# Local attention layers: the last inverse norms move from ScalarE's square root to VectorE, and the first tile's softmax moves forward

## The chip, the cores and the metric

The kernel runs on one core of a Trainium2 chip. The metric is the device time of one execution in microseconds; the time before is the median of three runs. Five engines matter, and each works through its own queue of instructions in order: TensorE (PE), VectorE (DVE), ScalarE (ACT), GpSimd (POOL) and SyncE (SP), which only issues DMAs. They meet through semaphores: an instruction may raise one when it is done, and a wait in a queue holds everything behind it in that queue.

## The reference, cut to what matters

The program computes two large layers for a batch of 4 sequences of 1024 tokens of width 128. The part that the change touches stands in the gate branch of the second layer: two local attention layers (`DEPTH = 2`), each with 8 heads of 64 channels and windows of 64 tokens that also see the window before.

```python
qkv = h @ wqkv
q, k, v = to_heads(split(qkv))
q = l2norm(q) * qs                       # q / max(|q|, 1e-12), for each token and head
k = l2norm(k) * ksc
q, k = rotary_xpos(q, k)
sim = einsum('bhwid,bhwjd->bhwij', q * 8, look_around(k))
attn = softmax(where(mask, -max, sim))   # 64 queries, 128 keys
o = einsum('bhwij,bhwjd->bhwid', attn, look_around(v))
x = x + o @ wo                           # then a GEGLU feed-forward part
```

The four sequences are worked one after the other and each passes two local layers, so the changed stretch runs 8 times in an execution.

## The kernel before, in words

A local layer is cut into T = 8 tiles of 128 tokens. It has two loops on each engine, written out by hand, and the order of the code is the order of each queue.

**The projection loop, tiles t = 0 to 7.** TensorE's `qkv(t)` multiplies a tile by the three weight blocks into two banks of PSUM for q and k and one for v. VectorE's `rotate(t)` multiplies q and k by the cosine and sine tables (lines 1228 and 1235), and GpSimd adds the two products (line 536). ScalarE squares q and k (line 746) and copies v out (line 747). VectorE sums the squares of each head (line 1260, its result `ssq`), and after every second tile takes the maximum with a floor (line 1265). ScalarE takes the square root of two tiles' sums (line 751), and VectorE's `inverse(k)` makes a reciprocal of it and one Newton step (lines 1242 to 1245). Only the keys need the inverse norm in place: GpSimd multiplies them by it (line 542). The queries' inverse norm is applied later, as the scale of the exponential. TensorE's `kq(t)` transposes a finished tile into two banks, first the queries' half, then the keys' half (line 1734), and ScalarE's `keep(t)` copies both halves out (lines 733 and 735). `kq(t)` runs four tiles behind the projection (`LAG = 4`), and each half of it waits until `keep(t - 1)` has emptied its bank.

**The score loop, u = 0 to 11.** TensorE's `scores(u)` first adds the mask and then multiplies queries by keys (both told as line 1412, as all its matmuls are). VectorE's `top(u)` takes the maximum of each row (line 1274) and multiplies it by minus the inverse norm (line 1276). ScalarE runs eight exponentials for a tile, one per head, each with its sum (line 765). VectorE then divides by the sums (lines 1301 and 1303), TensorE transposes the weights (line 1817), ScalarE and VectorE copy them out (lines 773 and 1329), TensorE multiplies by the values and by `wo`, and VectorE adds the result to x (line 1309).

**The seam between the two loops** is where the change lies. Before, ScalarE's queue there holds: `keep(2)`, square and v of tile 7, `keep(3)`, square root of tiles 6 and 7, a one-element exponential that brings in the exponential's table (line 753), `keep(4)`, the exponentials of tile 0, `keep(5)`, the exponentials of tile 1, `keep(6)`, and so on (`LATE = 3` tiles are kept within the score loop). VectorE's queue holds: rotation of tile 7, inverse norms of tiles 4 and 5, sums of squares of tiles 6 and 7, maximum with the floor, `top(0)`, inverse norms of tiles 6 and 7, `top(1)`. TensorE's queue holds: `qkv(7)`, `kq(3)`, `scores(0)`, `kq(4)`, `scores(1)`, `kq(5)`, `scores(2)`, `kq(6)` (`EARLY = 2`). GpSimd's queue holds: keys of tile 4, rotation sum of tile 7, keys of tiles 5, 6 and 7.

The exponentials' output `pl` lies in three buffers over the same memory as the rotated tiles 2, 3 and 4 (`qk_a`), which is free once their transposes are done.

Of the kernel before, what the change touches and what calls it, by code (L numbers as in the profile page):

```python
# [7 lines left out]
ACT = mybir.ActivationFunctionType  # L8
# [3 lines left out]
AX = mybir.AxisListType.X  # L12

B, N, W = 4, 1024, 128
P = 128
T = N // P
# [50 lines left out]
def build(nc, d, out):  # L67

    with ExitStack() as ctx:
# [489 lines left out]
        def _(act):  # L559
# [21 lines left out]
            with nc.Fori(0, B, engines=(act.engine,), hint_back_edge=True, head_slot={act.engine: 0}) as b:  # L581
# [139 lines left out]
                for l in range(DEPTH):  # L721
# [7 lines left out]
                    def keep(t):  # L729
# [5 lines left out]
                        act.copy(kT[:, :, WIN + P * t:WIN + P * t + P],  # L735
                                 PS[:, 7, :].rearrange("p (c n) -> p c n", c=4)).then_inc(S["kq"], 1)

                    for t in range(T + LAG + 1 - LATE):
                        u = l * T + t
                        if t >= LAG + 1:  # L740
                            keep(t - LAG - 1)
                        if t < T:
                            act.wait_ge(S["rotb"], u + 1)
                            if u >= 2:
                                act.wait_ge(S["ssq"], u - 1)
                            act.activation(qk_sq[l][t % 2], pair(2 * (t % 2)), ACT.Square).then_inc(S["sq"], 1)  # L746
                            act.copy(vl[:, t], PS[:, 4 + t % 2, :]).then_inc(S["vl"], 1)  # L747
                        if 2 <= t <= T and t % 2 == 0:
                            k = t - 2
                            act.wait_ge(S["ssq_ok"], u // 2)  # L750
                            act.activation(rq[:, k:k + 2], rqt[:, k:k + 2], ACT.Sqrt).then_inc(S["rq0"], 1)
                        if t == T:
                            act.activation(sc[0:1, 9:10], ident[0:1, 0:1], ACT.Exp)
                    for u in range(T + 4):
                        n = T * l + u
                        if u < T:
                            if 1 <= u <= LATE:
                                keep(T - LATE + u - 1)
                            act.wait_ge(S["ml"], n + 1)
                            if n >= 3:  # L760
                                act.wait_ge(S["pt_ps"], 2 * (n - 2))
                            for r in range(2):
                                for c in range(4):
                                    h = 2 * c + r
                                    act.activation(pl[:, n % 3, r, c], PS[:, 2 * (n % 2) + r, KEYS * c:KEYS * c + KEYS],  # L765
                                                   ACT.Exp, bias=ml[:, n % 2, r, c:c + 1], scale=rq[:, u, h:h + 1],
                                                   accum_out=sl[:, n % 3, r, c:c + 1]).then_inc(S["p_exp"], 1)
                        if 2 <= u <= T + 1:
                            m = n - 2
                            if m >= 2:  # L770
                                act.wait_ge(S["o_lps"], m - 1)
                            act.wait_ge(S["pt_ps"], 2 * m + 1)
                            act.copy(pt[:, m % 2, 0], PS[:, 4, :].rearrange("p (c n) -> p c n", c=4)).then_inc(S["pt"], 1)  # L773
                        if 3 <= u <= T + 2:
                            q = n - 3
                            act.wait_ge(S["o_lps"], q + 1)
                            if q >= 2:
                                act.wait_ge(S["ol_ps"], q - 1)
                            act.copy(olT[:, q % 2], PS[:, 6, :].rearrange("p (c n) -> p c n", c=4))\  # L779
                                .then_inc(S["olT"], 1)  # L780
# [26 lines left out]
        def _(dve):  # L807
# [120 lines left out]
            with nc.Fori(0, B, engines=(dve.engine,), hint_back_edge=True, head_slot={dve.engine: 0}) as b:  # L928
# [287 lines left out]
                for l in range(DEPTH):  # L1216
# [21 lines left out]
                    def inverse(k):  # L1238

                        y, v, w = rq[:, k:k + 2], rqt[:, k:k + 2], ssq[:, k:k + 2]  # L1240
                        dve.wait_ge(S["rq0"], (l * T + k) // 2 + 1)
                        link(dve.reciprocal(y, y))
                        link(dve.scalar_tensor_tensor(w, y, -0.5, y, ALU.mult, ALU.mult))
                        link(dve.tensor_tensor(w, w, v, ALU.mult))
                        dve.scalar_tensor_tensor(y, w, 1.5, y, ALU.add, ALU.mult).then_inc(S["rqe"], 2)

                    for t in range(T + 1):
                        u = l * T + t
                        if t < T:
                            rotate(t)  # L1250
                        if l == 0 and t == 0:
                            rows_back(1)
                        if l == 0 and t == 1:
# [8 lines left out]
                        if 2 <= t and t % 2 == 0:  # L1262
# [4 lines left out]
                    def top(u):  # L1267

                        n = T * l + u
                        sv = PS[:, 2 * (n % 2):2 * (n % 2) + 2, :].rearrange("p r (c k) -> p r c k", k=KEYS)  # L1270
                        dve.wait_ge(S["s_lps"], n + 1)
                        if n >= 2:
                            dve.wait_ge(S["p_exp"], 8 * (n - 1))
                        link(dve.tensor_reduce(ml[:, n % 2], sv, AX, ALU.max))  # L1274

                        dve.scalar_tensor_tensor(ml[:, n % 2], ml[:, n % 2], -1.0,
                                                 rq[:, u, 0:HL].rearrange("p (c r) -> p r c", r=2),
                                                 ALU.mult, ALU.mult).then_inc(S["ml"], 1)

                    top(0)  # L1280
                    inverse(T - 2)

                    def own_half(t):

# [11 lines left out]
                    for u in range(T + 6):  # L1296
                        n = T * l + u
                        if 2 <= u <= T + 1:
                            m = n - 2
                            dve.wait_ge(S["p_exp"], 8 * (m + 1))  # L1300
                            link(dve.reciprocal(rl[:, m % 3], sl[:, m % 3]))
                            v = pl[:, m % 3]
                            dve.tensor_tensor(v, v, bc(rl[:, m % 3], [P, 2, 4, KEYS], 3), ALU.mult).then_inc(S["pn"], 1)
                        if 1 <= u < T:
                            top(u)
                        if u >= 6:
# [103 lines left out]
        def _(pe):  # L1410
# [22 lines left out]
            with nc.Fori(0, B, engines=(pe.engine,), hint_back_edge=True, head_slot={pe.engine: 0}) as b:  # L1433
# [277 lines left out]
                for l in range(DEPTH):  # L1711
# [52 lines left out]
                    for t in range(T):  # L1764
# [13 lines left out]
                            out_products()  # L1778
                        if l == 0 and t == 3:
                            pe.wait_ge(S["op_rd"], 1)  # L1780
                        if t >= LAG:
                            kq(t - LAG)
                    for t in range(EARLY):
                        scores(t)
                        kq(T - LAG + t)
                    for u in range(T + 4):
                        n = T * l + u
# [22 lines left out]
                        if 2 <= u <= T + 1:  # L1810
                            m = n - 2
                            pe.wait_ge(S["pn"], m + 1)
                            for r in range(2):
                                if m:
                                    pe.wait_ge(S["ptd" if r else "pt"], m)
                                for c in range(4):
                                    ins = pe.transpose(PS[:, 4 + r, P * c:P * c + P], pl[:, m % 3, r, c], ident[:])
# [197 lines left out]
```

## Time and profile before

| what | value |
|---|---|
| median of 3 runs | 2427.04 us (2421.03 to 2428.21) |
| profiled execution, its own time | 2423.78 us |
| its span, first to last instruction | 2421.7 us |
| mean granted TensorE clock | 0.939 |
| busy: PE, DVE, ACT, POOL | 86%, 78%, 60%, 25% |

The span is what the trace covers; the 2.1 us between it and the execution's own time lie around the program. A granted clock of 1.00 is 2.4 GHz, 0.50 is 1.2 GHz. In rows of a timeline the bracket tells how long the engine sat idle ahead of the instruction and what ended that. All times of a timeline are microseconds from the span's start. The first local layer of the first sequence, which the rows below show, runs from about 414 to 520 us.

### The profile page before, as it was taken

To read this page: it belongs to the slowest core of one execution; us is meant where nothing else is said; L and a number is where in the kernel's file an instruction comes from. 1 tells how busy PE (TensorE), PEld (TensorE's weight loads), DVE (VectorE), ACT (ScalarE), POOL (GpSimd) and SP (SyncE) were. 2 spreads that over 40 slices of the span, in tenths; PEclk is the share of its full clock that TensorE was granted. 3 is DMA by queue.
4 is the path that set the end of the run, shared out by engine and by line. 5 is a ranking of instruction groups with operands and counts; after the bars stand their busy time and mean duration, and the time that the engine had idled before them with its cause. 6 is when DMAs were issued, how large, how long until landed. Compare 5 with 4: busy or idle time off the path is not lost.

```text
span 2421.7 us, 49342 instructions
## 1 busy us (share of the span) xinstructions
PE 2072.6 (86%) x18320; PEld 1204.0 (50%) x18320; DVE 1894.7 (78%) x3719; ACT 1456.9 (60%) x3090; POOL 602.0 (25%) x480
## 2 busy tenths in 40 slices
PE   5997899787799699978779969987788996998877
PEld 4675233556467423364647733336464772334645
DVE  7746998887765699878776579987877558998786
ACT  4333698748334379784733438967563344996765
POOL 2632000332252200124134310031504330004050
PEclk9999799999899789999989979999998996999999
DMA  4001200100000210101000031010100003001010
GB/s 159 1 1 53 55 12 11 30 21 19 19 1 1 77 33 9 21 21 32 16 10 1 1 86 27 9 30 12 33 14 9 1 1 93 20 12 34 5 34 22
DMA packets 63896, 63.28 MB, mean 26 GB/s; under 512 B 22000, under 2 KB 49200, under 8 KB 63152
## 3 DMA queue, kind: packets, MB, share of 16 engines
q1 hardware_dynamic: 60472, 57.27, 9.4%
q8 instruction: 148, 2.42, 0.4%
q10 hardware_dynamic: 3192, 2.90, 0.4%
q14 instruction: 84, 0.69, 0.1%
HBM read 24.68 MB, written 15.01 MB: 16 GB/s over the span
## 4 chain that ended last, share of the span: by engine, by line
PE 52%; DVE 22%; ACT 17%; issue 5%; DMA 2%; SPq 1%; POOL 0%; DVEq 0%; ACTq 0%
PE PS L1412 50%; ACT arena L765 9%; DVE arena L1150 3%; DVE arena L1260 2%; ACT arena L708 2%; DVE s_at L1235 1%; DVE arena L1228 1%; PE PS L1430 1%; DMA tmp<-xf 1%; DVE tmp L1235 1%; ACT arena L773 1%; DVE arena L1353 1%; ACT arena L733 1%; ACT arena L735 1%; ACT x_in L779 1%
## 5 line engine op out<-in xcount | busy, mean ns | idle before, releaser
L1412 PE MATMUL PS<-arena 128*32 128x256 f32 (+5 forms) x11328 | 788.8, 327 | 115.2 <-DVE arena L1150 24.2
L1412 PEld LDWEIGHTS PS<-arena 128*32 128x32 f32 (+5 forms) x11328 | 349.1, 118 | 554.0 <-ACT arena L708 203.0
L1150 DVE TENSOR_REDUCE arena<-PS 128x2 f32<-128x1024 f32 x512 | 592.5, 1216 | 29.5 <-PE PS L1412 28.3
L708 ACT ACTIVATE arena<-PS 128x512 f32<-128x512 f32 x944 | 513.2, 596 | 93.2 <-PE PS L1412 69.5
L661 ACT ACTIVATE arena<-PS 128x512 f32<-128x512 f32 x256 | 150.7, 597 | 244.2 <-PE PS L1412 244.1
L1412 PEld LDWEIGHTS PS<-w2e,arena 128*128 128x128 f32 x2048 | 246.0, 192 | 50.7 <-issue 49.8
L1113 DVE TENSOR_TENSOR arena<-PS,arena 128x512 f32<-128x512 f32 x128 | 86.2, 688 | 208.5 <-PE PS L1412 208.1
L1412 PE MATMUL PS<-w2e,arena 128*128 128x128 f32 x2048 | 247.7, 275 | 0.3
L765 ACT ACTIVATE arena<-PS,arena 128x128 f32<-128x128 f32 x512 | 236.5, 626 | 0.0
L511 POOL TENSOR_TENSOR zz<-zz,arena 128x512 f32<-128x512 f32 x104 | 135.2, 1300 | 265.6 <-DVE arena L1113 236.7
L1412 PE MATMUL PS<-wqkv,arena 128*128 128x512 f32 x384 | 176.8, 598 | 21.7 <-ACT arena L747 21.7
L765 ACT ACTIVATION_READ_ACCUMULATOR arena<-PS,arena 128x1 f32 x512 | 176.2, 374 | 0.0
L520 POOL CAST arena<-arena 128x32 bf16<-128x32 f32 x64 | 13.4, 209 | 624.4 <-DVE arena L1169 624.4
L547 POOL TENSOR_TENSOR tmp<-xf,b2f 128x1024 f32<-128x1024 f32 x8 | 18.8, 2355 | 422.3 <-ACT xT L785 422.3
L1412 PE MATMUL PS<-xT,w1e 128*128 128x512 f32 x256 | 120.5, 596 | 0.2
L1412 PE MATMUL PS<-x,w1e 128*128 128x512 f32 x256 | 120.5, 596 | 0.1
L1412 PEld LDWEIGHTS PS<-wqkv,arena 128*128 128x128 f32 x384 | 67.8, 190 | 97.5 <-issue 75.8
L500 POOL TENSOR_TENSOR arena<-arena 128x1024 f32<-128x1024 f32 x32 | 75.2, 2349 | 131.3 <-ACT arena L610 122.6
L1412 PE MATMUL PS<-xT,wf 128*128 128x512 f32 (+1 forms) x192 | 89.8, 597 | 3.8 <-ACT xT L785 3.8
L746 ACT ACTIVATE arena<-PS 128x1024 f32<-128x1024 f32 x32 | 32.7, 1023 | 97.4 <-DVE s_at L1235 97.4
L1274 DVE TENSOR_REDUCE arena<-PS 128x8 f32<-128x1024 f32 x64 | 78.2, 1223 | 10.8 <-PE PS L1412 10.6
L1412 PE MATMUL PS<-xT,vw 128*128 128x512 f32 x128 | 77.6, 737 | 9.2 <-ACT arena L598 9.2
(308 smaller groups left out, 3301.1 us busy)
## 6 DMA issues: line engine op xcount, KB each, us to landing
arena<-arena SPq DMA_DIRECT2D x120, 128.0 KB, 2.3
scr_q<-arena SPq DMA_DIRECT2D x40, 128.0 KB, 2.4
scr_k<-arena SPq DMA_DIRECT2D x40, 128.0 KB, 2.4
arena<-scr_k SPq DMA_DIRECT2D x24, 200.0 KB
arena<-scr_q SPq DMA_DIRECT2D x24, 192.0 KB
scr_m<-arena SPq DMA_DIRECT2D x256, 1.0 KB
x_in<-in_x SPq DMA_DIRECT2D x5, 512.0 KB, 4.5
arena<-scr_m SPq DMA_DIRECT2D x128, 2.0 KB
```

What stands on the lines that cost most here:

```text
L500: pool.tensor_tensor(ub[:, c % 2], vsb[:, c % 2], bsb[:, c % 2], ALU.mult).then_inc(S["ub"], 1)
L511: pool.tensor_tensor(zz[:, half], src[:, half], ym[:, m % 4], ALU.add).then_inc(S["z"], 1)
L661: act.activation(hs[:, n % 8], PS[:, up_bank("up", k, c), :], ACT.Silu).then_inc(S["hs"], 1)
L708: act.activation(pb[:, n % 8, HALF * r:HALF * r + HALF], PS[:, (2 * n + r) % 3, :], ACT.Exp)\
L746: act.activation(qk_sq[l][t % 2], pair(2 * (t % 2)), ACT.Square).then_inc(S["sq"], 1)
L765: act.activation(pl[:, n % 3, r, c], PS[:, 2 * (n % 2) + r, KEYS * c:KEYS * c + KEYS], ACT.Exp, bias=ml[:, n % 2, r, c:c + 1], scale=rq[:, ...
L1113: dve.tensor_tensor(ym[:, m % 4], PS[:, 4 + m % 4, :].rearrange("p (t w) -> p t w", w=W), bc(comb[:, half, e // EPG, e % EPG], [P, T // 2, ...
L1150: dve.tensor_reduce(mxp[:, blk % 2, 2 * s:2 * s + 2, t, hf], PS[:, at:at + 2, :], AX, ALU.max)\
L1235: ins = dve.tensor_tensor(o, v, bc(w, [P, 2, HL, DL // 2], 2), ALU.mult)
L1260: dve.tensor_reduce(ssq[:, k], qk_sq[l][k % 2].rearrange("p (h c) -> p h c", c=DL), AX, ALU.add).then_inc(S["ssq"], 1)
L1274: link(dve.tensor_reduce(ml[:, n % 2], sv, AX, ALU.max))
L1412: return pe.matmul(o, w, v, start=start, stop=stop, **kw)
```

## The change

1. The inverse norms of tiles 6 and 7 no longer use ScalarE's square root. A new function `inverse_last` on VectorE computes them from the floored sums with the integer seed of the inverse root (a shift and a multiply-add on the bits) and three Newton steps: eleven small instructions of 128 x 32 in place of a reciprocal and three. ScalarE keeps the three square roots for tiles 0 to 5.
2. ScalarE's one-element exponential, with its table load, moves from behind the last square root (t = 8) to behind the third one (t = 6).
3. TensorE's `scores(0)` moves from behind `kq(3)` to right behind `qkv(7)`.
4. VectorE's `top(0)` moves from behind the last maximum to right behind the rotation of tile 7, ahead of the inverse norms of tiles 4 and 5.
5. ScalarE's exponentials of tile 0 (now the function `weights(0)`) move from behind `keep(4)` to right behind square and v of tile 7, ahead of `keep(3)`.
6. The buffer of a tile's exponentials is picked by the tile's number in its layer (u % 3) instead of its number over both layers (n % 3), so that tile 0's always lies where rotated tile 2 was.

```diff
 ACT
+                    def weights(u):
+                        n = T * l + u
+                        act.wait_ge(S["ml"], n + 1)
+                        if n >= 3:
+                            act.wait_ge(S["pt_ps"], 2 * (n - 2))
+                        for r in range(2):
+                            for c in range(4):
+                                h = 2 * c + r
+                                act.activation(pl[:, u % 3, r, c], PS[:, 2 * (n % 2) + r, KEYS * c:KEYS * c + KEYS],
+                                               ACT.Exp, bias=ml[:, n % 2, r, c:c + 1], scale=rq[:, u, h:h + 1],
+                                               accum_out=sl[:, u % 3, r, c:c + 1]).then_inc(S["p_exp"], 1)
                     for t in range(T + LAG + 1 - LATE):
...
                             act.copy(vl[:, t], PS[:, 4 + t % 2, :]).then_inc(S["vl"], 1)
-                        if 2 <= t <= T and t % 2 == 0:
+                        if t == T - 1:
+                            weights(0)
+                        if 2 <= t < T and t % 2 == 0:
                             k = t - 2
                             act.wait_ge(S["ssq_ok"], u // 2)
                             act.activation(rq[:, k:k + 2], rqt[:, k:k + 2], ACT.Sqrt).then_inc(S["rq0"], 1)
-                        if t == T:
+                        if t == T - 2:
                             act.activation(sc[0:1, 9:10], ident[0:1, 0:1], ACT.Exp)
                     for u in range(T + 4):
                         n = T * l + u
-                        if u < T:
-                            if 1 <= u <= LATE:
+                        if 1 <= u < T:
+                            if u <= LATE:
                                 keep(T - LATE + u - 1)
...
+                            weights(u)
 DVE
+                    def inverse_last():
+                        y, v, w = rq[:, T - 2:T], rqt[:, T - 2:T], ssq[:, T - 2:T]
+                        dve.wait_ge(S["ssq_ok"], T // 2 * (l + 1))
+                        rsqrt(v, y, w, 2)
+                        link(dve.scalar_tensor_tensor(w, y, -0.5, y, ALU.mult, ALU.mult))
+                        link(dve.tensor_tensor(w, w, v, ALU.mult))
+                        dve.scalar_tensor_tensor(y, w, 1.5, y, ALU.add, ALU.mult).then_inc(S["rqe"], 2)
                     for t in range(T + 1):
                         u = l * T + t
                         if t < T:
                             rotate(t)
+                        if t == T - 1:
+                            top(0)
...
-                    top(0)
-                    inverse(T - 2)
+                    inverse_last()
 PE
                             out_products()
                         if l == 0 and t == 3:
                             pe.wait_ge(S["op_rd"], 1)
+                        if t == T - 1:
+                            scores(0)
                         if t >= LAG:
                             kq(t - LAG)
                     for t in range(EARLY):
-                        scores(t)
+                        if t:
+                            scores(t)
                         kq(T - LAG + t)
```

`rsqrt`, which the kernel already has for other norms, is:

```python
link(dve.tensor_scalar(t_.bitcast(I32), v.bitcast(I32), 1, None, ALU.logical_shift_right))
link(dve.tensor_scalar(y.bitcast(I32), t_.bitcast(I32), -1.0, RSQRT_SEED, ALU.mult, ALU.add))
for _ in range(steps):
    link(dve.scalar_tensor_tensor(t_, y, -0.5, y, ALU.mult, ALU.mult))
    link(dve.tensor_tensor(t_, t_, v, ALU.mult))
    link(dve.scalar_tensor_tensor(y, t_, 1.5, y, ALU.add, ALU.mult))
```

`link` makes VectorE wait for the instruction just issued before it takes the next.

## Rows read from the trace of the kernel before

**Rows 1.** Page, chain that ended last: share of the span by engine.
```profile
PE 52%; DVE 22%; ACT 17%; issue 5%; DMA 2%; SPq 1%; POOL 0%; DVEq 0%; ACTq 0%
```

**Rows 2.** Chain of waits by time (start us, us, what), first local layer.
```profile
454.27 3.48 ACT arena L765 x16
```

**Rows 3.** Timeline of ACT (start us, us, engine, line, operation), the same layer.
```profile
419.51 1.02 ACT L746 ACTIVATE arena<-PS 128x1024 f32<-128x1024 f32 x1 [5.18 <-DVE s_at L1235]
...
445.74 0.24 ACT L751 ACTIVATE arena<-arena 128x32 f32<-128x32 f32 x1
...
448.06 1.02 ACT L746 ACTIVATE xf<-PS 128x1024 f32<-128x1024 f32 x1 [1.12 <-DVE tmp L1235]
448.98 0.58 ACT L747 COPY arena<-PS 128x512 f32<-128x512 f32 x1
...
451.58 0.23 ACT L751 ACTIVATE arena<-arena 128x32 f32<-128x32 f32 x1 [1.04 <-DVE arena L1265]
...
453.23 0.56 ACT L733 COPY arena<-PS 128x512 f32<-128x512 f32 x1
...
458.60 0.45 ACT L765 ACTIVATE arena<-PS,arena 128x128 f32<-128x128 f32 x1
...
492.61 0.59 ACT L773 COPY arena<-PS 128x512 f32<-128x512 f32 x1 [1.98 <-PE PS L1817]
```

**Rows 4.** Timeline of PE, the same layer.
```profile
442.71 2.74 PE L1412 MATMUL PS<-wqkv,arena 128*128 128x512 f32 x6
446.60 1.12 PE L1734 MATMUL PS<-ident,arena 128*128 128x128 f32 x8 [1.15 <-ACT arena L733]
...
447.89 1.04 PE L1412 MATMUL PS<-arena 64*64 64x128 f32 x32
...
453.93 1.11 PE L1734 MATMUL PS<-ident,xT 128*128 128x128 f32 x8 [1.41 <-ACT arena L733]
457.90 0.64 PE L1412 MATMUL PS<-band,identb 64*64 64x512 bf16 x4 [2.86 <-ACT arena L765]
...
460.18 1.97 PE L1734 MATMUL PS<-ident,tmp 128*128 128x128 f32 x8
```

**Rows 5.** Timeline of DVE, the same layer.
```profile
446.75 1.28 DVE L1235 TENSOR_TENSOR tmp<-PS,rot_s 128x512 f32<-128x512 f32 x2
...
448.84 0.19 DVE L1245 SCALAR_TENSOR_TENSOR arena<-arena 128x32 f32<-128x32 f32 x1
...
451.32 0.22 DVE L1265 TENSOR_REDUCE arena<-arena 128x32 f32<-128x64 f32 x1
...
452.71 0.85 DVE L1276 SCALAR_TENSOR_TENSOR arena<-arena 128x8 f32<-128x8 f32 x1
...
454.39 0.19 DVE L1245 SCALAR_TENSOR_TENSOR arena<-arena 128x32 f32<-128x32 f32 x1
...
455.75 1.04 DVE L1276 SCALAR_TENSOR_TENSOR arena<-arena 128x8 f32<-128x8 f32 x1
```

**Rows 6.** Timeline of POOL, the same layer.
```profile
452.51 1.04 POOL L542 TENSOR_TENSOR xT<-xT,arena 128x512 f32<-128x512 f32 x1
...
455.72 1.04 POOL L542 TENSOR_TENSOR x_in<-x_in,arena 128x512 f32<-128x512 f32 x1
```

**Rows 7.** Groups by line over the span: count | busy us, mean ns | idle us before.
```profile
L1243 DVE SCALAR_TENSOR_TENSOR arena<-arena 128x32 f32<-128x32 f32 x32 | 6.1, 192 | 1.1
L1274 DVE TENSOR_REDUCE arena<-PS 128x8 f32<-128x1024 f32 x64 | 78.2, 1223 | 10.8 <-PE PS L1412 10.6
```

**Rows 8.** Single lines: durations ns min/median/max, first and last start us.
```profile
L753 ACT ACT_TABLE_LOAD  x8: 1283/1283/1283, 451.8 to 2340.6; - x8
L1276 DVE SCALAR_TENSOR_TENSOR arena<-arena x64: 166/168/1041, 452.7 to 2372.2; 128x8 f32<-128x8 f32 x64
```

**Rows 9.** Stretches (us, PE busy (x), granted clock, DMA share, GB/s), layers one and eight.
```profile
456.00:457.00 1.00, 0.00 (x0) 0.75 0.00 0
459.33:460.33 1.00, 1.00 (x21) 0.50 0.00 0
463.00:464.00 1.00, 1.00 (x35) 0.84 0.00 0
2348.07:2349.07 1.00, 1.00 (x9) 0.50 0.00 0
```

More of the change, by code:

```diff
@@ L755, in _ @@
                         n = T * l + u
-                        if u < T:
-                            if 1 <= u <= LATE:
+                        if 1 <= u < T:
+                            if u <= LATE:
                                 keep(T - LATE + u - 1)
[L759 to L767, printed above, removed]
+                            weights(u)
                         if 2 <= u <= T + 1:
@@ L1240, in inverse, with top @@
                         y, v, w = rq[:, k:k + 2], rqt[:, k:k + 2], ssq[:, k:k + 2]
-                        dve.wait_ge(S["rq0"], (l * T + k) // 2 + 1)
+                        dve.wait_ge(S["rq0"], (T // 2 - 1) * l + k // 2 + 1)
                         link(dve.reciprocal(y, y))
+                        link(dve.scalar_tensor_tensor(w, y, -0.5, y, ALU.mult, ALU.mult))
+                        link(dve.tensor_tensor(w, w, v, ALU.mult))
+                        dve.scalar_tensor_tensor(y, w, 1.5, y, ALU.add, ALU.mult).then_inc(S["rqe"], 2)
+                    def top(u):
+                        n = T * l + u
+                        sv = PS[:, 2 * (n % 2):2 * (n % 2) + 2, :].rearrange("p r (c k) -> p r c k", k=KEYS)
+                        dve.wait_ge(S["s_lps"], n + 1)
+                        if n >= 2:
+                            dve.wait_ge(S["p_exp"], 8 * (n - 1))
+                        link(dve.tensor_reduce(ml[:, n % 2], sv, AX, ALU.max))
+                        dve.scalar_tensor_tensor(ml[:, n % 2], ml[:, n % 2], -1.0,
+                                                 rq[:, u, 0:HL].rearrange("p (c r) -> p r c", r=2),
+                                                 ALU.mult, ALU.mult).then_inc(S["ml"], 1)
+                    def inverse_last():
+                        y, v, w = rq[:, T - 2:T], rqt[:, T - 2:T], ssq[:, T - 2:T]
+                        dve.wait_ge(S["ssq_ok"], T // 2 * (l + 1))
+                        rsqrt(v, y, w, 2)
                         link(dve.scalar_tensor_tensor(w, y, -0.5, y, ALU.mult, ALU.mult))
@@ L1300, in _ @@
                             dve.wait_ge(S["p_exp"], 8 * (m + 1))
[L1301 to L1303 removed]
+                            link(dve.reciprocal(rl[:, (u - 2) % 3], sl[:, (u - 2) % 3]))
+                            v = pl[:, (u - 2) % 3]
+                            dve.tensor_tensor(v, v, bc(rl[:, (u - 2) % 3], [P, 2, 4, KEYS], 3), ALU.mult).then_inc(S["pn"], 1)
                         if 1 <= u < T:
```

12 lines of the change are left out of this document (1 added, 11 removed).

## The prediction, as it was put on record before the kernel was built

> **What bounds the kernel now.** I read the chain that ended last, by engine, then in order of time through one local layer, then the timeline of each engine over its seam. Over the whole span PE holds most of the chain [rows 1], but the seam is not PE's: there the chain passes from VectorE's sums to ScalarE, and from the first exponential on it stays on ScalarE [rows 2]. The ACT timeline shows it. ScalarE waits 1.12 us for the rotation of tile 7 and 1.04 us for the last maximum; behind the square root at 451.58 it has no idle time until 492.61 [rows 3]. So the end of the layer moves by as much as ScalarE's first exponential of **tile 1** moves, which now starts at 458.60 [rows 3]. From there to 492.61 the code is unchanged, and an engine without a gap can make nothing up. I therefore follow each engine to that instruction. All eight passes carry the same instructions, so a layer's difference counts eight times.
>
> **The change part by part, in the first layer's clock.**
>
> *ScalarE's head.* Before, from the square root at 451.58 to `keep(4)` at 453.23 is 1.65 us, 1.28 of it the table load [rows 3, 8]. Now this stretch follows the square root at 445.74 instead, so `keep(2)` starts at 447.39. A keep pair takes 0.945: from 453.23 to 458.60 lie two pairs and eight exponentials of 3.48 together [rows 2, 3]. Tile 7's square starts at 448.34 instead of 448.06, v's copy at 449.26, and the exponentials can start 0.47 (one copy) later, at 449.73. Its two old idle gaps of 1.12 and 1.04 cover most of the load, and the square of tile 7, 0.28 late, is read by VectorE only after 451. That the square runs under the exponential's table is no new load: the first tiles' squares in this layer run right behind the attention's exponentials, and no load precedes the one at 419.51 [rows 3].
>
> *Tile 0's scores and maximum.* `qkv(7)` ends at 445.45; the scores take from 447.72 to 448.93, some 1.25 [rows 4], so they are ready at 446.8. VectorE's rotation of tile 7 ends at 448.03 [rows 5], the maximum takes 1.22 and its product 0.17 [rows 7, 8]: ready at 449.45. GpSimd is idle then. So the exponentials of tile 0 do start at 449.73, some 4.4 us earlier than now, and end at 453.2. If only ScalarE counted, three keep pairs would follow and tile 1 would start at 453.2 + 2.84 = 456.05, 2.55 early.
>
> *What is queued behind them.* `keep(3)` now stands behind the exponentials: it starts at 453.2, where `keep(4)` started before, one tile behind the old order. TensorE's `kq(4)` waits for `keep(3)` to empty its bank, `scores(1)` stands behind `kq(4)`, and `kq(5)` behind that; ScalarE needs `kq(5)` for `keep(5)`, and that comes ahead of tile 1's exponentials. So a path through TensorE is late next. `kq(4)` follows its keep by 0.70 (453.23 to 453.93 [rows 3, 4]) and starts at 453.9. At full clock: `kq(4)` 1.1, scores 1.25, `kq(5)` 1.1 give 457.35; the second half's copy starts 0.14 later and the exponentials 0.47 after that: 457.96, a gain of 0.64.
>
> *The clock on that path.* Before, TensorE is idle 2.86 us ahead of 457.90 [rows 4]. Its granted clock falls from 1.00 to 0.50 at about 456.5, 1.5 after it went idle, and stays there to about 463.3, though work had begun at 457.90; all eight layers show the low level there, of which the first and the last stand in the rows [rows 9]. At 1.2 GHz scores with their mask take from 457.90 to 460.18, 2.28, and a `kq` 1.97 [rows 4]. There this was harmless; the late ones had slack against ScalarE. Now `kq(3)` ends at about 449.2 (0.70 behind `keep(2)`, plus 1.1) and TensorE has nothing until 453.9, an idle time of 4.7, longer than the one that lowered the clock. All of the path at the low level: 453.9 + 1.97 + 2.28 + 1.97 = 460.1, tile 1's exponentials at 460.75: 2.15 late. The best that the rows allow with a fall: down at 450.7 (1.5 behind the last work), up 6.8 later as before, at 457.5; then `kq(4)` and seven tenths of the scores are slow, the rest 0.4 and 1.1: 459.0, exponentials at 459.6, 1.0 late. I take the middle, 1.55, since the fall may come anywhere in the gap.
>
> *VectorE's eleven steps.* A step of 128x32 takes 0.192 + 0.034 [rows 7]; eleven, the seeds priced alike, 2.49. Everything behind the moved maximum is 1.4 later on VectorE and GpSimd, so the last maximum ends at 452.94 (451.32 + 0.22 + 1.4 [rows 5]), and alone the steps would end at 455.4. But two-input VectorE work stood still while GpSimd ran: the product of `top` takes 0.17 alone, and 0.85 and 1.04 in the rows, ending with GpSimd's 452.51 + 1.04 and 455.72 + 1.04 [rows 5, 6, 8]. GpSimd's rotation sum of tile 7 and keys of tile 5 are now at 451.6 to 454.95, over the steps. Bounds: 455.4 if such small steps are spared, 457.4 if all wait; I take 457.1, since the rows show waiting. Between the end of the inverse norms and the end of tile 1's product lay 454.58 to 456.79, 2.21, with the same GpSimd work in it [rows 5, 6]. So its maximum is ready at 459.3, which is 0.7 late by itself. The Trainium skill (SBUF — State Buffer, "SBUF: two separate sides") says the same more widely: the pair of ports that VectorE and GpSimd share is locked for the whole instruction, also for VectorE's work with two SBUF inputs against a GpSimd instruction that reads SBUF. The trace agrees for the 128x8 product (1.04 in place of 0.17) and does not show the small steps beside GpSimd. By the page every Newton step waits and the maximum is ready at 459.6; if only the product waits, it is ready soon after the scores of tile 1, and TensorE's path alone decides.
>
> *The rest.* One square root less on ScalarE (0.23) lies in what moved. No DMA is moved; v's copies feed theirs 0.28 later with microseconds to spare. The buffer index changes no count.
>
> **Sum.** Both late paths meet at tile 1's exponentials, so the later one counts: 1.55 a layer, 8 x 1.55 = 12.4. Against the profiled execution, 2423.78 + 12.4 = 2436.2. The runs' median lies 3.3 above that execution; on its footing it is 2439.5. I give 2438, between the two.
>
> **The rivals.**
> - *The low clock comes back.* TensorE, finished early with tile 1, idles again until the next exponentials end, falls again, and the weights' transposes (about twice 1.1 at the low level) hold ScalarE's next copy: 1.1 more a layer, 2.65 x 8 = 21, 2445 (2448 on the median's footing). For it: the order of work there has little slack. Against it: idle gaps below 2 us on this path so far left the clock at 1.00 (1.41 ahead of 453.93).
> - *The clock stays up.* Then the eleven steps decide: 0.7 x 8 = 5.6, 2429 (2433). Against it: rows 9.
> - *Neither holds* (the other side). If the clock is up when `kq(4)` starts and GpSimd spares the small steps, tile 1 starts at 457.96, with its maximum ready before: 8 x -0.64 = -5, 2419 (2422). It decides from the point where `kq(5)` ends before 458.0.
> - *ScalarE's own account.* If TensorE could run ahead, 8 x -2.55 = -20, 2403 (2407). It speaks against it that `kq(4)` must wait for `keep(3)`, as `kq(5)` waited for `keep(4)` at 453.93 [rows 4].
> - *It doesn't do what it says.* If the maximum of tile 0 comes too late for ScalarE, the queue is the old one with a wait in front; each us of it is another 8. The working leaves 0.28 us between the maximum (449.45) and ScalarE's being ready (449.73), so it costs little.
>
> **How the numbers follow.** Forecast 0.57, low clock again 0.10, clock up 0.13, neither 0.10, ScalarE's account 0.10. A change of this kernel can be told from none at about 0.3%, 7.3 us. The forecast's own range is 8 to 17 (2435 to 2444 on the median's footing): nearly all slower. Clock up and neither are within it; ScalarE's account is faster. With a little for what I have not seen: slower 0.60, same 0.26, faster 0.14. The range takes in all but ScalarE's account: 2422 to 2450.
>
> **What would show it.** Right: the first exponentials of tile 0 near 449.7 and no square root or table load between the last square and `keep(3)`; then ScalarE idle ahead of `keep(4)` and `keep(5)`, on TensorE's transposes; a granted clock of 0.50 in the stretch of `scores(1)`; small steps of `inverse_last` with one of 1 us or more; tile 1 starting 1 to 2.2 later against the rotation of tile 7 than the 10.6 of now. Wrong: ScalarE without idle time between tile 0 and tile 1, or `kq(4)` and `kq(5)` taking 1.1 each, or the score loop from tile 1 on having new gaps of its own.

## The result, and the profile after

The changed kernel takes 2450.12 us (median of 4 runs, 2448.44 to 2450.72) against 2427.62 for the kernel before in the same comparison (2421.03 to 2431.78): ratio 1.0094, 95% interval 1.0075 to 1.0112. It is slower, by about twice what was forecast (2438). The profiled execution has a span of 2447.8 us and a granted clock of 0.934, against 2421.7 and 0.939: 26.1 us more to explain.

The page's chain by engine answers to [rows 1]: a little more of the end is TensorE's (55% for 52%).

```profile
PE 55%; DVE 20%; ACT 15%; issue 5%; DMA 2%; POOL 1%; SPq 1%; DVEq 0%; ACTq 0%; POOLq 0%
```

The seam of the first layer, which runs 0.68 later than before by then. ACT's timeline, against [rows 3] (line numbers have moved: L759 is the square, L733 and L735 a keep pair, L747 the exponentials):

```profile
445.03 1.02 ACT L759 ACTIVATE arena<-PS 128x1024 f32<-128x1024 f32 x1 [2.24 <-DVE s_at L1242]
...
449.02 1.01 ACT L759 ACTIVATE xf<-PS 128x1024 f32<-128x1024 f32 x1
450.40 0.45 ACT L747 ACTIVATE arena<-PS,arena 128x128 f32<-128x128 f32 x1
...
453.89 0.57 ACT L733 COPY arena<-PS 128x512 f32<-128x512 f32 x1
455.72 0.58 ACT L733 COPY arena<-PS 128x512 f32<-128x512 f32 x1 [0.78 <-PE PS L1751]
...
459.90 0.58 ACT L733 COPY arena<-PS 128x512 f32<-128x512 f32 x1 [2.74 <-PE PS L1751]
...
461.23 0.46 ACT L747 ACTIVATE arena<-PS,arena 128x128 f32<-128x128 f32 x1
```

ScalarE no longer waits ahead of tile 7's square, and tile 0's exponentials run from 450.40 to 453.89. Then it waits for TensorE's `kq(4)` and again, 2.74 us, for `kq(5)`, with tile 1's exponentials behind that. PE's timeline, against [rows 4]:

```profile
448.78 1.11 PE L1751 MATMUL PS<-ident,arena 128*128 128x128 f32 x8 [1.30 <-ACT arena L733]
454.60 1.94 PE L1751 MATMUL PS<-ident,arena 128*128 128x128 f32 x8 [4.71 <-POOL x_in L536]
456.47 0.64 PE L1429 MATMUL PS<-band,identb 64*64 64x512 bf16 x4
456.90 1.92 PE L1429 MATMUL PS<-arena 64*64 64x128 f32 x32
458.75 1.97 PE L1751 MATMUL PS<-ident,xT 128*128 128x128 f32 x8
```

`kq(4)`, `scores(1)` and `kq(5)`, each 1.7 to 1.9 times as long as at full clock. The bracket names GpSimd, but GpSimd's sum was done at 454.53; `kq(4)` follows the first half of `keep(3)` (453.89 + 0.57) by 0.14. The clock is in the stretches (us; busy time of PE, PEld, DVE, ACT and POOL, each with its number of instructions; granted clock; DMA share; GB/s; PEld is TensorE's load of weights). The last of them lies in the second layer's projection loop, and under it stands the kernel before there, at 1.00:

```profile
450.00:451.00 1.00, 0.00 (x0) 0.00 (x0) 0.83 (x6) 1.00 (x5) 0.00 (x0) 0.72 0.00 0
455.00:456.00 1.00, 1.00 (x7) 1.00 (x6) 0.93 (x3) 0.28 (x1) 0.53 (x1) 0.50 0.00 0
459.00:460.00 1.00, 1.00 (x6) 1.00 (x6) 1.00 (x1) 0.10 (x1) 0.86 (x1) 0.50 0.00 0
532.70:533.70 1.00, 1.00 (x2) 0.42 (x2) 0.60 (x1) 1.00 (x2) 1.00 (x1) 0.50 0.90 205
```
```profile
530.00:531.00 1.00, 1.00 (x3) 0.38 (x2) 0.67 (x1) 1.00 (x2) 1.00 (x2) 1.00 0.90 207
```

VectorE's timeline, against [rows 5], and under it GpSimd's, against [rows 6]:

```profile
453.59 0.98 DVE L868 TENSOR_SCALAR arena<-arena 128x32 int32<-128x32 int32 x1
454.60 0.97 DVE L869 TENSOR_SCALAR arena<-arena 128x32 int32<-128x32 int32 x1
455.60 0.19 DVE L871 SCALAR_TENSOR_TENSOR arena<-arena 128x32 f32<-128x32 f32 x1
...
457.48 0.19 DVE L1274 SCALAR_TENSOR_TENSOR arena<-arena 128x32 f32<-128x32 f32 x1
458.89 1.22 DVE L1261 TENSOR_REDUCE arena<-PS 128x8 f32<-128x1024 f32 x1 [1.22 <-PE PS L1429]
```
```profile
452.19 2.34 POOL L536 TENSOR_TENSOR x_in<-x_in,tmp 128x1024 f32<-128x1024 f32 x1
454.49 1.04 POOL L542 TENSOR_TENSOR xT<-xT,arena 128x512 f32<-128x512 f32 x1
```

The eleven steps end at 457.67, and still the maximum of tile 1 waits 1.22 for `scores(1)`. So TensorE's path decides.

**Where the 26.1 us are.** Three spans, each worked from starts in ScalarE's timeline. *Seam*: square of tile 6 to the first exponential of tile 1; 14.25 in all layers before, 16.16 to 16.20 in the first and 15.81 to 15.84 in the second layers after: 14.1 together. *Loop*: square of tile 0 to square of tile 6. It is 24.84 in the first layers of both kernels, but in the second layers 23.49 before and 25.19 after: 4 x 1.70 = 6.8. *The rest* is 5.2: 0.7 ahead of the first layer, 4.5 behind the second layers' last exponentials, mostly in the large layers (418.9, 417.6, 419.0 between two sequences before; 419.8 to 420.1 after). Between tile 1's first and the layer's last exponential nothing changed: 30.11. Loop and rest hold no changed instruction. The rest may be no effect of the change: the traced execution of the kernel before lies 3.8 below the median of 2427.62, that of the kernel after 0.3 above its own, so that of the medians' 22.5 only 1.6 are left to it.

### The profile page after: what moved, and what is told of

Its sections match the earlier page's. It is cut to its first block, busy times and chain, and to the rows that moved or that the text cites. A ratio compares the mean times of both kernels' runs of the same rounds, so it can differ in the third digit from the quotient of the medians.

```text
span 2447.8 us, 49390 instructions
## 1 busy us (share of the span) xinstructions
PE 2082.1 (85%) x18320; PEld 1211.6 (49%) x18320; DVE 1898.9 (78%) x3775; ACT 1456.8 (60%) x3082; POOL 601.7 (25%) x480
## 4 chain that ended last, share of the span: by engine, by line
PE 55%; DVE 20%; ACT 15%; issue 5%; DMA 2%; POOL 1%; SPq 1%; DVEq 0%; ACTq 0%; POOLq 0%
PE PS L1429 52%; ACT arena L747 8%; DVE arena L1157 3%; ACT arena L708 2%; PE PS L1751 1%; DVE s_at L1242 1%; DVE arena L1291 1%; DVE arena L1235 1%; PE PS L1447 1%; DMA tmp<-xf 1%; DVE tmp L1242 1%; ACT arena L780 1%; POOL x_in L536 1%; DVE arena L1370 1%; ACT x_in L786 1%
## 5 line engine op out<-in xcount | busy, mean ns | idle before, releaser
L747 ACT ACTIVATE arena<-PS,arena 128x128 f32<-128x128 f32 x512 | 237.2, 638 | 0.0
L1429 PE MATMUL PS<-wqkv,arena 128*128 128x512 f32 x384 | 183.5, 617 | 21.7 <-ACT arena L760 21.7
L747 ACT ACTIVATION_READ_ACCUMULATOR arena<-PS,arena 128x1 f32 x512 | 179.7, 386 | 0.0
L759 ACT ACTIVATE arena<-PS 128x1024 f32<-128x1024 f32 x32 | 32.7, 1023 | 104.2 <-DVE s_at L1242 104.2
```

What stands on the lines that cost most here:

```text
L747: act.activation(pl[:, u % 3, r, c], PS[:, 2 * (n % 2) + r, KEYS * c:KEYS * c + KEYS], ACT.Exp, bias=ml[:, n % 2, r, c:c + 1], scale=rq[:, ...
L1429: return pe.matmul(o, w, v, start=start, stop=stop, **kw)
```

## The experiments

All timings are beside runs of the kernel before (medians 2426.3 to 2428.1). "Slow loops" are second layers, of four, whose loop took 24.8 to 25.2 in place of 23.5. Seams and loops come from the one profiled execution of each kernel, medians from all of its runs.

| kernel | median us | ratio (95%) | seam us | slow loops |
|---|---|---|---|---|
| before | 2427.6 | 1 | 14.25 | 0 |
| after | 2450.1 | 1.0094 (1.0075 to 1.0112) | 15.8 to 16.2 | 4 |
| e1 warm seam | 2443.2 | 1.0066 (1.0050 to 1.0081) | 14.90 | 0 |
| e2 warm second loop | 2436.9 | 1.0047 (1.0029 to 1.0066) | 14.9 to 16.2 | 0 |
| e3 both | 2449.6 | 1.0098 (1.0081 to 1.0114) | 14.91 | 0 |
| e15 e1 and more waits | 2441.4 | 1.0062 (1.0048 to 1.0075) | 14.91 | 0 |
| e17 three and two | 2439.0 | 1.0047 (1.0032 to 1.0061) | 14.90 | 0 |
| e18 five in the seam | 2452.9 | 1.0104 (1.0087 to 1.0121) | 14.90 | 2 |
| e16 before, 0.94 late | 2437.2 | 1.0034 (1.0022 to 1.0047) | 15.19 | 2 |
| e8 before, 1.88 late | 2449.7 | 1.0091 (1.0075 to 1.0106) | 16.13 | 4 |
| e9 before, 3.5 late | 2458.7 | 1.0123 (1.0106 to 1.0141) | 17.76 | 1 |
| e7 inverse norms alone | 2429.0 | 1.0010 (0.9999 to 1.0021) | 13.87 | 1 |
| e4 keep(3) first | 2438.9 | 1.0047 (1.0034 to 1.0060) | 14.90 | 1 |
| e5 top(1) first | 2450.4 | 1.0096 (1.0080 to 1.0111) | 15.1 to 16.2 | 3 |
| e6 both of these | 2424.2 | 0.9989 (0.9980 to 0.9998) | 12.2 to 13.0 | 4 |
| e10 e6, warm second loop | 2422.1 | 0.9984 (0.9974 to 0.9995) | 12.2 to 13.1 | 0 |
| e11 e6, inverse(4) first | 2440.1 | 1.0050 (1.0038 to 1.0062) | 14.94 | 2 |
| e12 e11, warm second loop | 2434.6 | 1.0030 (1.0018 to 1.0042) | 14.5 to 15.0 | 0 |
| e13 e11, GpSimd waits | 2422.5 | 0.9978 (0.9969 to 0.9988) | 12.2 to 12.9 | 2 |
| e14 e13, warm second loop | 2420.0 | 0.9969 (0.9957 to 0.9980) | 12.2 to 12.9 | 0 |

**TensorE kept busy with matmuls that nobody reads.** e1, in the changed kernel's seam, TensorE:

```diff
+                    pe.wait_ge(S["rotb"], T * l + T)
+                    pe.wait_ge(S["sq"], T * l + T)
+                    for _ in range(4):
+                        mm(PS[:, 2, :], ident[:], res["w1e"][:, 0:HALF])
                     for t in range(EARLY):
```


> The changed kernel (median 2450.1 us) with four 128x512 float32 matmuls, whose result nobody reads, in TensorE's gap between kq(3) and kq(4) of each local layer. Theory (the path keep(3), kq(4), scores(1), kq(5), keep(5) is late because TensorE runs it at the low clock): granted clock 1.00 through the seam, kq(4) and kq(5) 1.1 us each instead of 1.95, and tile 1's first exponential comes 1.0 to 1.3 us earlier in its layer, held then by the maximum of tile 1; 8 to 10 us less in all, 2440 to 2442, if the second layers' projection loops stay as slow as they are. Rival (the order alone, the clock is hidden): within 1 us a layer of noise, 2450.

e2, in the second layers' projection loop; e3 has both edits:

```diff
+                        if l and t == 1:
+                            for _ in range(2):
+                                mm(PS[:, 7, :], ident[:], res["w1e"][:, 0:HALF])
```


> The changed kernel with two such matmuls in TensorE's gap between qkv(1) and qkv(2) of each second local layer, where the trace shows the clock at 0.50 in all four sequences (7.1 us for two tiles of projections instead of 5.4). Theory (this low clock is a second loss, outside the seam): projection loop of the second layers 1.7 us shorter each, 4 x 1.7 = 6.8 us, 2443. Rival (the loop is held by something else, ScalarE or VectorE): 2450.

> Both sets of matmuls at once. Theory of two separate low-clock losses: the sum, 15 to 17 us less than the changed kernel, 2433 to 2435, still above the kernel before (2427.6) by the late maximum of tile 1. Rival (one loss that shows up in either place): no more than the better of the two, about 2441.

With a warm seam `kq(4)` to `kq(5)` take 1.1, 1.3 and 1.1, and the granted clock is 1.00 there in all eight layers. TensorE in e1:

```profile
452.56 1.11 PE L1751 MATMUL PS<-ident,arena 128*128 128x128 f32 x8 [0.75 <-POOL x_in L536]
453.61 0.41 PE L1429 MATMUL PS<-band,identb 64*64 64x512 bf16 x4
453.85 1.04 PE L1429 MATMUL PS<-arena 64*64 64x128 f32 x32
454.82 1.09 PE L1751 MATMUL PS<-ident,xT 128*128 128x128 f32 x8
```

VectorE ends last now. ScalarE's first exponential of tile 1 in e1, and VectorE's product that it waits for, which stands beside GpSimd:

```profile
457.90 0.46 ACT L747 ACTIVATE arena<-PS,arena 128x128 f32<-128x128 f32 x1 [1.31 <-DVE arena L1263]
```
```profile
456.82 1.04 DVE L1263 SCALAR_TENSOR_TENSOR arena<-arena 128x8 f32<-128x8 f32 x1
```

The seam falls to 14.90: the low clock is worth 1.3 in a first layer there and 0.9 in a second, and VectorE's steps 0.65, for which "the clock stays up" had said 0.7. The second layers' loops come back to 23.49 although e1 did nothing in them; so do they in e2, whose second seams fell to 14.9 to 15.1 although it did nothing in those: its span is 13.1 shorter than the changed kernel's, where 6.8 was said. What is done in one place moves the clock in another. e1's median is still 17 us over before's: in its profiled execution, its fastest run, 5.2 of 10.6 is the seam and 3.6 a low clock in the second layers' score loop (31.02 for 30.11). Some 3 us of the 17 lie outside the span: between it and the execution's own time are about 5 us in e1, e15 and e17, and about 2 in the kernel before, in e3 and in e18. No run shows why.

e3 had the seams and the loops that it was meant to have, but neither time that was expected of it: it lost about 4.2 us at each of the three turns of the loop over sequences. Three runs on that: e15 (the second wait of e1 issued three times), e17 (three matmuls in the seam and two in the second loop, eight a sequence as in e1), e18 (five in the seam, ten as in e3).

> The changed kernel with four unread matmuls in the seam, and the wait ahead of them issued three times instead of once: four instructions more on TensorE in each sequence, no more work. Theory (at the turn of the loop over sequences TensorE's next code was not there, and how much of it is missing goes by the number of its instructions): TensorE's idle time ahead of the first transpose of sequences 2 to 4 is 9.3 instead of 5.1, and the time 2443 + 3 x 4.2 = 2456. Rival (the 4.2 us belong to the two matmuls in the second layers): 5.1, and 2443.

> The changed kernel with three unread matmuls in each seam and two in the second layers' loop: eight in a sequence, as many as in the run with four in each seam alone. If their number decides: TensorE's idle time ahead of the first transpose of sequences 2 to 4 is 5.1, and the time 2449.6 - 12.6 = 2437 (2433 to 2443). If their place in the second layers decides: 9.3, and 2446 to 2452. Tile 1's exponentials 14.9 behind the square of tile 6 if three keep the clock up, some 16 if not.

> The changed kernel with five unread matmuls in each seam and none in the second layers' loop: ten in a sequence. If their number decides: 9.3 us ahead of the first transpose of sequences 2 to 4 and 2443 + 12.6 = 2456 (2450 to 2458). If their place decides: 5.1 and 2437 to 2446. Tile 1's exponentials 14.9 behind the square of tile 6, as with four.

TensorE's first transpose of the next sequence, in e17 and under it in e18:

```profile
634.74 1.97 PE L1447 MATMUL PS<-ident,xn 128*128 128x128 f32 x8 [5.11 <-SPq L447]
```
```profile
1242.16 1.97 PE L1447 MATMUL PS<-ident,xn 128*128 128x128 f32 x8 [9.39 <-issue]
```

Ten matmuls a sequence cost it in either placing, and eight don't (5.1 in e1 too). e15, at 5.1 as well, doesn't tell their number from the amount of code: its trace has only 8 instructions more than e1's over the four sequences (49534 for 49526), two a sequence and not the four that were said, where e3's has 32 more (49558), for each unread matmul is two MATMUL records and two weight loads. The amount of code is what the profile's pages speak for. The queue that brings instructions moved more in e3 and e18 than in every other kernel here; e17's page, and under it e18's (transfers, MB, share of 16 engines' span):

```profile
q8 instruction: 148, 2.42, 0.4%
```
```profile
q8 instruction: 151, 2.47, 0.4%
```

These are some 16 KB more at each of the three turns. In e3 and e18 one such transfer falls into each of the six idle times ahead of the first transpose, 2.7 us before it; in the kernel before, e1, e15 and e17 none falls there. The Trainium skill (Runtime: NRT & Kernel Launch, "Instruction fetch mechanics") says that a taken branch to code that isn't at hand waits for it to be fetched. The runs agree with it in the place, the loop's turn, and in the additional transfer; that TensorE's wait ended with it the profile doesn't tell ("issue"), and no run changed the amount of code without matmuls by as much.

**The kernel before, only later.** e8: linked one-element exponentials ahead of tile 1's exponentials. e16 has four, e9 fifteen.

```diff
+                            if u == 1:
+                                for _ in range(8):
+                                    link(act.activation(sc[0:1, 9:10], ident[0:1, 0:1], ACT.Exp))
                             act.wait_ge(S["ml"], n + 1)
```


> The kernel before, with eight tiny linked exponentials (one element each) ahead of tile 1's exponentials on ScalarE: some 2 us late a layer, by nothing but time. Theory (the clock in the second layers' projection loop depends on when that loop arrives, not on the changed code): 8 x 2 = 16 us plus up to 6.8 us from the second layers, 2444 to 2451, with the second layers' loops at 0.50 in some places. Rival (the changed code slows the second layers' loop itself): 16 us only, 2444, and every projection loop as long as before (23.5 us from the first to the seventh square).

> The kernel before with fifteen linked one-element exponentials ahead of tile 1's exponentials instead of eight: by the 1.88 us that eight cost, about 3.5 us late in each layer. Two readings of the second layers' projection loop, which went from 23.49 to 25.19 with 1.88 us of lateness and unchanged code. If a late seam is what lowers the clock there, the loop stays at 25.19 or more and the time is 2426 + 28 + 7 = 2461 or above. If the clock there goes by where the same work happens to fall in the chip's granting of it, twice the lateness need not cost it: the loop may be back at 23.49 and the time at 2454 to 2457, that is the plain 8 x 3.5.

> The kernel before with four linked one-element exponentials ahead of tile 1's exponentials: about 0.94 us late in each layer. If any lateness costs the second layers' loop its clock: the loop 25.1 and the time 2427 + 7.5 + 6.8 = 2441. If it goes by where the loop falls: 23.49 is as likely, and 2432 to 2437.

The matmuls of `qkv(2)` and `qkv(3)` in the first sequence's second layer, on TensorE's timeline, in the kernels before, after, e8 and e9:

```profile
528.81 5.42 PE L1412 MATMUL PS<-wqkv,arena 128*128 128x512 f32 x12 [2.19 <-ACT arena L747]
```
```profile
531.44 7.11 PE L1429 MATMUL PS<-wqkv,arena 128*128 128x512 f32 x12 [2.19 <-ACT arena L760]
```
```profile
531.38 7.11 PE L1415 MATMUL PS<-wqkv,arena 128*128 128x512 f32 x12 [2.19 <-ACT arena L747]
```
```profile
532.48 5.42 PE L1415 MATMUL PS<-wqkv,arena 128*128 128x512 f32 x12 [2.19 <-ACT arena L747]
```

The same twelve matmuls behind the same idle time of 2.19, at either level of the clock. 1.88 us of lateness alone make the kernel before as slow as the changed one, with all four loops slow and 26.1 us on its span; twice the lateness brings three loops back, and half of it two. The medians of e9 and e16 decide nothing: 2458.7 lies between e9's two readings, 2437.2 at the edge of e16's second. So the changed code isn't needed for the low clock there, and more lateness doesn't bring more of it. That leaves where the work falls, by exclusion and from one traced execution of each. The Trainium skill (TensorE: Matmul & The Clock Gate, Part 1) says that the gate's own rhythm runs on regardless of when a kernel starts; these runs fit that, though none tests it by itself. Which shift is lucky no run let me tell ahead.

**What the seam is bound by.** e7: points 1 and 2 of the change in the kernel before, tile 0 left where it was (VectorE's part of the edit):

```diff
                     top(0)
-                    inverse(T - 2)
+                    inverse_last()
```


> The kernel before with the first two points of the change alone: VectorE's inverse_last in place of the last square root, and the exponential's table load two tiles earlier; scores, maximum and exponentials of tile 0 stay where they were. Theory (the inverse norms are not what made the changed kernel slow): keep(4) is no longer behind a square root and a table load, but VectorE's steps end later; tile 1 starts between 0.5 earlier and 0.5 later than the 14.25 of before, 2420 to 2432. Rival (the eleven steps beside GpSimd are the price): tile 1 1 or more later, 2436 or more.

The seam is 0.38 shorter, the time the same: the inverse norms on VectorE alone are not what made the changed kernel slow. e4 puts `keep(3)` back ahead of tile 0's exponentials, e5 tile 1's maximum ahead of `inverse_last`, e6 does both. Here and below only a call's new place is shown; its old place is taken out:

```diff
                         if t == T - 1:
+                            keep(T - LAG - 1)
                             weights(0)
```
```diff
+                    top(1)
                     inverse_last()
```


> The changed kernel with keep(3) moved back ahead of tile 0's exponentials; the rest of the change stays. Theory (the path keep(3), kq(4), scores(1), kq(5) at the low clock makes tile 1 late, and the lateness itself costs the second layers' projection loop its clock): kq(4) then follows kq(3) within about a microsecond and the granted clock there stays at 1.00; from the square of tile 6 to the first exponential of tile 1 the 16.20 / 15.84 of the changed kernel fall to 14.1 to 14.4, where VectorE's eleven steps and the maximum behind them end last (ScalarE alone would allow 11.3); the second layers' loop goes back from 25.19 to 23.49. Time near the kernel before: 2422 to 2432. Rival (VectorE's steps and the shared port are the real price): the seam stays at 15.8 or more and the time above 2445.

> The changed kernel with tile 1's maximum ahead of inverse_last on VectorE. Theory (TensorE's path is what is late): scores(1) still end near 458.8, so the maximum cannot start earlier; tile 1's exponentials stay at 15.8 to 16.2 behind the square of tile 6, and the inverse norms of tiles 6 and 7, now behind that maximum, come 3 or more later, near 462 to 463, which makes GpSimd's keys and kq(6) late: 0 to 1.5 more a layer, 2448 to 2462. Rival (VectorE's eleven steps hold the maximum): tile 1 starts 1.4 or more earlier a layer, 2430 to 2438.

> Both moves together. Theory: with the transposes early and the maximum of tile 1 ahead of the eleven steps, only ScalarE's own queue is left: tile 1's exponentials 11.3 to 12.3 behind the square of tile 6 (14.25 in the kernel before). The inverse norms come some 1.4 later, so kq(6) is about 1.3 late for keep(6), and 1 to 2 us a layer remain as the gain: 2408 to 2420. Rival (it is the eleven steps, wherever they stand): what is gained at tile 1 is lost again at tile 2, 2422 to 2430.

e4 takes TensorE's path away and lands on the same 14.90 as e1, with ScalarE waiting 2.60 for tile 1's product:

```profile
462.67 0.46 ACT L747 ACTIVATE arena<-PS,arena 128x128 f32<-128x128 f32 x1 [2.60 <-DVE arena L1264]
```

14.1 to 14.4 took that product at 0.17, and beside GpSimd's keys it took 1.04. The clock did not stay at 1.00 as expected: in the first layer it fell to 0.50 at 454.15 and came back at 457.57, ahead of `kq(5)`. e4's median of 2438.9 misses 2422 to 2432. Of the 16.5 on its span the seams explain 5.2, one slow loop 1.7, and 4.4 go between tile 1 and the last exponentials. e5 agrees with its theory in time and, but for 15.1 to 15.7 in three layers, in the seam: the steps alone were not what held tile 1. With both, the seam is 12.2 to 13.0, 1.2 to 2.1 shorter than before, and the kernel gains 0.1%: a time in the rival's range. Tile 2 gives back some, as the rival said (1.36 of waiting for `kq(6)` in the first layer), but all four loops are slow besides, 1.6 to 1.7 each. e10 warms these:

> The kernel with keep(3) ahead of tile 0's exponentials and tile 1's maximum ahead of inverse_last, and two unread matmuls of 128x512 in TensorE's gap behind qkv(1) of the second layers. Theory (that kernel's gain of 1 to 2 us a layer is paid back as 1.6 to 1.7 us of low clock in the second layers' loop): the loop goes from 25.1 back to 23.49 and the time falls by 5 to 7 us to 2416 to 2420. Rival (the low clock only moves to another place): 2422 to 2427.

The loops come back and 2 us with them, not 5 to 7: the rival, the low clock moves on. e11 puts VectorE's inverse norms of tiles 4 and 5 ahead of tile 0's maximum in e6, to bring GpSimd's keys of tile 4 and `kq(4)` forward; e12 adds e2's matmuls:

```diff
                             inverse(t - 3)
+                        if t == T - 1:
+                            top(0)
```


> The same kernel without those matmuls, but the inverse norms of tiles 4 and 5 ahead of tile 0's maximum on VectorE. Theory: GpSimd's keys of tile 4 come 1.3 earlier, and with them the second half of kq(4), scores(1), tile 1's maximum, inverse_last and the keys of tile 6; the wait of 1.36 that ScalarE had ahead of keep(6)'s second half goes, and tile 2's exponentials come 1.2 to 1.6 earlier a layer: 2412 to 2418, less or more by the clock of the second layers' loop. Rival (tile 0's maximum, 1.1 later, holds ScalarE): tile 0's exponentials start 0.3 or more later and 2422 to 2428.

> Both: inverse norms of tiles 4 and 5 ahead of tile 0's maximum, and the two unread matmuls in the second layers. Theory: the gains add up, second layers' loop 23.49, 2406 to 2412. Rival (the time follows the granted clock of the large layers between, which each new timing sets anew): 2414 to 2425 although the seam and the loop are as early as said.

Both missed. Tile 0's product, in e11, and ScalarE behind it:

```profile
450.52 2.35 DVE L1264 SCALAR_TENSOR_TENSOR arena<-arena 128x8 f32<-128x8 f32 x1
```
```profile
452.91 0.46 ACT L747 ACTIVATE arena<-PS,arena 128x128 f32<-128x128 f32 x1 [1.82 <-DVE arena L1264]
```

The product of 0.17 had come to stand beside GpSimd's rotation sum of 2.35. In e13 GpSimd waits for it; e14 adds e2's matmuls.

```diff
                             pool.wait_ge(S["rotb"], u + 1)
+                            if t == T - 1:
+                                pool.wait_ge(S["ml"], T * l + 1)
```


> The kernel with keep(3) and tile 1's maximum moved and the inverse norms of tiles 4 and 5 ahead of tile 0's maximum, in which GpSimd now waits for tile 0's product before it takes the rotation sum of tile 7. Theory (in the run before, the product of tile 0's maximum took 2.35 instead of 0.17 because it stood beside that sum, and this alone held tile 0's exponentials 1.8 us): the product takes 0.17, ScalarE has no wait ahead of tile 0's exponentials, these start 6.3 to 6.5 behind the square of tile 6 (8.24 there), tile 1's 12.2 to 13, and ScalarE does not wait for keep(6); 2408 to 2418. Rival (the order is at fault: tile 0's maximum is simply later): 7.4 or more behind the square of tile 6 and 2425 or more.

> The same with the two unread matmuls in the second layers' loop. Theory: the loop at 23.49 in all four, 2404 to 2414. Rival (the clock is lost elsewhere): no faster than the kernel without them.

The same product and the first seed on VectorE, and ScalarE's first exponential, which no longer waits, in e13:

```profile
451.20 0.17 DVE L1266 SCALAR_TENSOR_TENSOR arena<-arena 128x8 f32<-128x8 f32 x1
...
455.17 0.17 DVE L871 TENSOR_SCALAR arena<-arena 128x32 int32<-128x32 int32 x1
```
```profile
451.67 0.45 ACT L749 ACTIVATE arena<-PS,arena 128x128 f32<-128x128 f32 x1
```

So GpSimd's sum held it, not the order. e14 beats both kernels: 2420.0, ratio 0.9969 (0.9957 to 0.9980). But its seams are 14.9 shorter together in the profiled execution and its span only 6.2: 3.0 go between tile 1 and the last exponentials and 6.0 behind them, mostly in the large layers. The times of e13 and e14 are over what was expected of them, as e10's was, though their seams are as said.

## Why the forecast was too small

- **ScalarE's head, tile 0's scores and maximum, the queue behind: right.** From the square of tile 6 to tile 0's exponentials 5.37 were measured, where the working has 5.38 (449.73 less 419.51 + 24.84); `kq(4)` followed `keep(3)` by 0.71 (0.70 said).
- **The path that is late next: right.** ScalarE waits for `kq(4)` and `kq(5)`, not for the maximum.
- **The clock on that path: mis-sized.** "I take the middle, 1.55, since the fall may come anywhere in the gap." It had come before `kq(4)` began in all eight layers (at 450.4 in the first) and went only while `kq(5)` ran: 1.94 late in a first layer and 1.58 in a second, within the bounds of 1.0 and 2.15. 14.1 in place of 12.4.
- **VectorE's eleven steps: right, as a term.** Held by GpSimd, with the seam 0.65 late once TensorE was out of the way (e1, e4); 0.7 said. The rival built on it priced the seam, and not the time: 2433 said, 2439 and 2443 measured.
- **The step that failed**: "All eight passes carry the same instructions, so a layer's difference counts eight times." The seam's difference did count eight times, but the sum 8 x 1.55 has no term for anything outside the seam: it was put at nothing because no instruction there changes. In its place the second layers' loops took 6.8 us more, their `qkv(2)` and `qkv(3)` 7.11 in place of 5.42 at a granted clock of 0.50. e8 shows it for the loops without any changed code, and e2 shows that they come back when TensorE is kept busy ahead of them. The last 5.2 of the 26.1 stay open: no run took them apart, and most of them may be the difference between one execution and another.
- "The low clock comes back" was right in kind but put in the wrong place: score loops from tile 1 on take 30.11, as before. That its 2445 to 2448 lies nearer to the result than the forecast is luck.

## What to carry to other kernels

Follow a moved step to the engine that waits on it, and ask what that idle time does to TensorE's clock: here 4.7 us without work nearly doubled the next three steps. Where a kernel passes between the clock's two levels all along, the sum over the changed stretch is not the change of the time (15.0 us of waiting in e8 became 26.1): shift the old kernel by the expected amount, without the edit, and see what that alone costs. A short VectorE product that someone waits for must not come to stand beside a long GpSimd instruction; here one wait on GpSimd took 1.8 us off ScalarE's.

## What was not expected of the hardware

One-input int32 work on VectorE is held by GpSimd as two-input work is. The first seed, over all eight layers, in the kernel after (beside GpSimd) and in e13 (GpSimd idle); columns are min, median and max in ns:

```profile
L868 DVE TENSOR_SCALAR arena<-arena x8: 978/980/986, 453.6 to 2365.9; 128x32 int32<-128x32 int32 x8
```
```profile
L871 DVE TENSOR_SCALAR arena<-arena x8: 173/174/175, 455.2 to 2341.9; 128x32 int32<-128x32 int32 x8
```

The reduction of 128x1024 (L1291), one input too, was not: it takes 1.21 in all 64 instances of the kernel after, those that lie wholly beside GpSimd's sum among them. The prediction had counted the first seed as waiting, from rows of two-input work alone.
